# The opening of a fused attention and mixture-of-experts kernel, put in another order

## The reference, cut to what matters

```python
h = layernorm(x)                                  # no gain
qk, v = h @ Wqk, h @ Wv                           # split in heads of 16 channels
dot = qk_head @ qk_head.T                         # 16 x 16 for each head, summed over 2048 tokens
logits = (2 * dot - q2[:, None] - q2[None, :]) / sqrt(2048) * tau
out = (softmax(logits) @ v_head) -> tokens x 256, then @ Wo
x = x + layernorm(out)
h = layernorm(layernorm(x)) * ln_g + ln_b
expert(h) = (silu(h @ W1) * (h @ W3)) @ W2        # shared for all tokens, routed for the top two
x = x + layernorm(shared(h) + gated sum of the two routed experts, with a capacity)
```

## Time and profile before

| what | value |
|---|---|
| median of 3 runs | 1089.59 us (1089.08 to 1089.89) |
| profiled execution | 1089.17 us, its span 1087.4 us |
| TensorE busy | 1047.9 us, 96% of the span |
| VectorE, ScalarE, GpSimd busy | 656.2, 503.7, 385.4 us |
| granted TensorE clock over the span | 0.992 |

### The profile page before, as it was taken

The page is one execution under the profiler, slowest core; times in us unless marked ns, Lnnn a source line. Parts: engine busy times, 40 slices in busy tenths (PEclk is TensorE's granted clock), DMA queues, the critical chain, the costliest instruction groups (busy, mean ns, idle before and its releaser), DMA issues.

```text
span 1087.4 us, 19513 instructions
## 1 busy us (share of the span) xinstructions
PE 1047.9 (96%) x6863; PEld 958.0 (88%) x6863; DVE 656.2 (60%) x1714; ACT 503.7 (46%) x895; POOL 385.4 (35%) x347
## 2 busy tenths in 40 slices
PE   7998999999999999999999999999999999999985
PEld 6886888888888888889887899999999999999875
DVE  7768864677753678754786334545545463635686
ACT  4343444443434444353463334554546363545475
POOL 3112561114640104640117631434433343211385
PEclk9999999999999999999999999999999999999988
DMA  8222460242540234461134214434334242333799
GB/s 289 104 98 78 132 219 17 82 155 95 167 148 20 79 125 138 150 210 39 59 136 161 103 33 157 133 67 112 88 90 109 65 124 56 77 89 94 262 220 171
DMA packets 47229, 129.15 MB, mean 119 GB/s; under 512 B 10276, under 2 KB 17576, under 8 KB 47152
## 3 DMA queue, kind: packets, MB, share of 16 engines
q1 hardware_dynamic: 28656, 92.83, 25.5%
q0 software_dynamic: 18496, 35.35, 14.3%
HBM read 73.72 MB, written 54.40 MB: 118 GB/s over the span
## 4 chain that ended last, share of the span: by engine, by line
PE 82%; DVE 8%; POOL 4%; issue 3%; ACT 1%; DMA 1%; DVEq 0%; POOLq 0%; SPq 0%; ACTq 0%
PE bank L1136 25%; PE bank L1138 25%; PE bank L1137 25%; PE bank L1155 2%; POOL out_dram L906 2%; POOL sb_place_of L911 1%; DVE sb_stX L1427 1%; PE bank L1262 1%; PE bank L1315 1%; DVE sb_act L1734 1%; PE bank L1215 1%; PE bank L1274 1%; ACT sb_ln_o L965 1%; DMA sb_ysb<-in_L_ffn_W2s_dram 1%; PE bank L1185 1%
## 5 line engine op out<-in xcount | busy, mean ns | idle before, releaser
L1734 DVE TENSOR_TENSOR sb_act<-bank,sb_act 128x512 f32<-128x512 f32 (+2 forms) x240 | 148.6, 619 | 347.8 <-PE bank L1138 330.5
L1136 PE MATMUL bank<-sb_h_hi,sb_wup_lo 128*128 128x512 f32 (+2 forms) x960 | 354.7, 369 | 3.3 <-ACT sb_act L1061 2.1
L1138 PE MATMUL bank<-sb_h_hi,sb_wup_hi 128*128 128x512 f32 (+2 forms) x960 | 350.0, 365 | 0.0
L1137 PE MATMUL bank<-sb_h_lo,sb_wup_hi 128*128 128x512 f32 (+2 forms) x960 | 349.7, 364 | 0.0
L1061 ACT ACTIVATE sb_act<-bank 128x512 f32<-128x512 f32 (+2 forms) x240 | 129.8, 541 | 378.1 <-PE bank L1138 358.4
L1136 PE MATMUL bank<-sb_wdn_hi,sb_act_lo 128*128 128x256 f32 (+1 forms) x848 | 245.5, 290 | 5.1 <-ACT sb_ysb L1043 4.4
L1138 PE MATMUL bank<-sb_wdn_hi,sb_act_hi 128*128 128x256 f32 (+1 forms) x848 | 239.2, 282 | 0.0
L1137 PE MATMUL bank<-sb_wdn_lo,sb_act_hi 128*128 128x256 f32 (+1 forms) x848 | 239.0, 282 | 0.0
L1136 PEld LDWEIGHTS bank<-sb_h_hi,sb_wup_lo 128*128 128x128 f32 x960 | 181.0, 189 | 24.4 <-DVE sb_act L1734 2.5
L1138 PEld LDWEIGHTS bank<-sb_h_hi,sb_wup_hi 128*128 128x128 f32 x960 | 180.6, 188 | 22.6
L1137 PEld LDWEIGHTS bank<-sb_h_lo,sb_wup_hi 128*128 128x128 f32 x960 | 181.2, 189 | 17.1
(11 more groups left out here) (265 smaller groups left out, 1238.5 us busy)
## 6 DMA issues: line engine op xcount, KB each, us to landing
sb_xin<-in_L_ffn_W_dram SPq DMA_DIRECT2D x28, 512.0 KB, 3.6
sb_x<-in_L_attn_x_dram SPq DMA_DIRECT2D x16, 512.0 KB, 3.7
out_dram<-sb_x SPq DMA_DIRECT2D x16, 512.0 KB, 3.4
sb_xin<-in_L_attn_x_dram SPq DMA_DIRECT2D x14, 512.0 KB, 4.6
sb_xin<-in_x_turned_dram SPq DMA_DIRECT2D x14, 512.0 KB, 4.3
y_scratch<-sb_ysb SPq DMA_DIRECT2D x14, 512.0 KB, 4.2
sb_xn<-in_L_ffn_W_dram SPq DMA_DIRECT2D x14, 512.0 KB, 4.4
hT_scratch<-sb_hr SPq DMA_DIRECT2D x12, 512.0 KB, 2.7
```

Source lines behind the costliest of these rows:

```text
L1136: t_.matmul(o, a_lo, b_hi, start=start, stop=False, skip_group_check=True)
L1137: t_.matmul(o, a_hi, b_lo, start=False, stop=False, skip_group_check=True)
L1138: return t_.matmul(o, a_hi, b_hi, start=False, stop=stop, skip_group_check=True)
L1734: v.tensor_tensor(act[:, m % 3, 0:c.w], bank[(4 if c.wide and m % 2 else 0) + 1][:, 0:c.w], act[:, m % 3, 0:c.w], ALU.mult).then_inc(act_o ...
```

## The change

On TensorE, Wv's product leaves the head of the queue and becomes the step `wv_turn`, in two halves, at places 27 and 31 behind the Gram product; it reads Wv from another buffer and writes bank 1. In its old place stand 75 small products of ones. The counts of small products change: `m_dots` (18) and `m_rowdiag` (40) have none, the second half of `wv_turn` has 12. ScalarE copies `wvT` in `wv_keep`, at place 33.

For batch 0, VectorE normalizes tiles 0 and 1 of each group and makes a bias from mean and scale; ScalarE normalizes tiles 2 and 3 (`x_norm` on ScalarE). The Gram product waits tile by tile. The first group of x is loaded in two halves.

`x_keep` moves to places 13, 18, 27, 29 (from 16, 18, 24, 26); `x_low` to 17, 24, 35 and, for the fourth, to place 2 of step 0 (from 19, 20, 34, 34). `w_first` moves to 17, 21, 26, 28, 37, 37 (from 17, 19, 19, 29, 33, 34), `w_first_low` to 19, 24, 34, 44, 45, 47 (from 19, 24, 24, 34, 38, 38), `scale_taus` to 23 (from 25).

For step 0, ScalarE and VectorE share the first tile of h in another way, and the first row's products come as eight with the high part of h, then four with the remainder (`first_up`).

```diff
--- before.py
+++ after.py
...
@@ -456,7 +462,7 @@
         X_FIRST_AT = (("x_stats", (8, 9, 11, 13)), ("x_norm", (10, 12, 14, 15)), ("x_gram", (10, 12, 14, 15)),
-                      ("x_turned", (14, 14, 14, 15)), ("x_keep", (16, 18, 24, 26)), ("x_low", (19, 20, 34, 34)))
+                      ("x_turned", (14, 14, 14, 15)), ("x_keep", (13, 18, 27, 29)), ("x_low", (17, 24, 35, BEFORE + 2)))
         M_FIRST_AT = (20, 22, 22, 23, 24, 25, 26, 28, 30, 31, 32, 33, 34, 35, 36, 36, 37)
@@ -477,10 +483,12 @@
         put(0, -BEFORE, 0, zip(M_STEPS, M_FIRST_AT))
-        put(0, -BEFORE, 0, [("scale_taus", 25)])
-        for j, at in enumerate((17, 19, 19, 29, 33, 34)):
+        put(0, -BEFORE, 0, [("scale_taus", 23), ("wv_keep", 33)])
+        put(0, -BEFORE, 0, [("wv_turn", 27)])
+        put(0, -BEFORE, 1, [("wv_turn", 31)])
+        for j, at in enumerate((17, 21, 26, 28, 37, 37)):
             put(0, -BEFORE, j, [("w_first", at)])
-        for j, at in enumerate((19, 24, 24, 34, 38, 38)):
+        for j, at in enumerate((19, 24, 34, 44, 45, 47)):
             put(0, -BEFORE, j, [("w_first_low", at)])
@@ -534,8 +542,9 @@
         def _(sp):
-            for k in range(2):
-                sp.dma_start(x2[:, k, :, :], x_t[k]).then_inc(xres_in[k], 16)
+            for landed, tiles in ((x_early, slice(0, GT // 2)), (xres_in[0], slice(GT // 2, GT))):
+                sp.dma_start(x2[:, 0, tiles, :], x_t[0][:, tiles, :]).then_inc(landed, 16)
+            sp.dma_start(x2[:, 1, :, :], x_t[1]).then_inc(xres_in[1], 16)
             for opened in (hT_ok, g_done, o_ok, m_act, lno_ok, x2_ok, *x2_out, u_ok, ut_ps, lg_ps,
...
@@ -925,6 +933,16 @@
+            def x_norm(b, q):
+                if b > 0:
+                    return
+                act_e.wait_ge(x_nb, q + 1)
+                x = x2[:, q, :, :] if q < 2 else xin[:, q % 2, :, :]
+                for t, done in ((2, xn_third), (3, xn_ok)):
+                    s.activation(xnorm[q % 2][:, t, :], x[:, t, :], ACT.Identity, scale=rstdX[:, q, t:t + 1],
+                                 bias=nbX[:, q % 2, t:t + 1]).then_inc(done, 1)
             def x_high(b, q):
@@ -968,26 +986,35 @@
+            def first_keep(k):
+                act_e.wait_ge(ut_ps, OPEN + k + 1)
+                act_e.wait_ge(vec_in, 48)
+                s.activation(h_hi[:, shared_chunk(0, 0).slot, k, :], bank[6 + k][:, :], ACT.Identity,
+                             scale=gcol[:, k:k + 1], bias=bcol[:, k:k + 1]).then_inc((first_hi, hhi_ok)[k], 1)
+                if k == 1:
+                    s.activation(hfull[:, 1, :], bank[7][:, :], ACT.Identity,
+                                 scale=gcol[:, 1:2], bias=bcol[:, 1:2]).then_inc(hT_ok, 1)
             def u_keep(k):
                 def step(b, q):
-                    if opens(b, q) and k == 1:
+                    if opens(b, q):
+                        first_keep(k)
                         return
...
                     act_e.wait_ge(lg_ps, OPEN + b * GB + q)
-                    if b == 0 and q == 0:
-                        act_e.wait_ge(vec_in, 48)
                     if q == 0:
...
                         act_e.wait_ge(h_out, OPEN + b * H_LOADS + 16 * (q - 1))
-                    if opens(b, q):
-                        s.activation(h_hi[:, shared_chunk(0, 0).slot, 0, :], bank[6][:, :], ACT.Identity,
-                                     scale=gcol[:, 0:1], bias=bcol[:, 0:1]).then_inc(first_hi, 1)
                     s.activation((hfull if q == 0 else hr)[:, k, :], bank[6 + k][:, :], ACT.Identity,
...
-            steps = {"x_high": x_high, "x_keep": x_keep, "m_gram": m_gram,
+            def wv_keep(b, q):
+                act_e.wait_ge(wvT_ps, KC)
+                s.activation(wvT[:, :, :].rearrange("p k d -> p (k d)"), bank[1][:, :], ACT.Copy).then_inc(wvT_ok, 1)
+            steps = {"x_norm": x_norm, "wv_keep": wv_keep, "x_high": x_high, "x_keep": x_keep, "m_gram": m_gram,
                      "m_keep_t": m_halves(tsb, (5, 4), 2, (1, 0)),
...
@@ -1143,10 +1162,10 @@
                 for t in range(GT):
-                    if b == 0 and t < GT - 1:
-                        pe.wait_ge(xn_tile, q * (GT - 1) + t + 1)
+                    if b == 0 and t < GT // 2:
+                        pe.wait_ge(xn_tile, q * (GT // 2) + t + 1)
                     elif b == 0:
-                        pe.wait_ge(xn_ok, OPEN + (q + 1))
+                        pe.wait_ge((xn_third, xn_ok)[t - 2], (0, OPEN)[t - 2] + (q + 1))
                     for k in range(KC):
...
@@ -1316,12 +1333,29 @@
+            def first_up(c):
+                pe.wait_ge(first_hi, 1)
+                pe.wait_ge(w_lo, 4)
+                for k, turned in ((0, first_hi), (1, hhi_ok)):
+                    pe.wait_ge(turned, 1)
+                    for which in range(2):
+                        for w in (wup_lo, wup_hi):
+                            t_.matmul(bank[which][:, :], w[c.wset][:, which, k, 0:P], h_hi[:, c.slot, k, :],
+                                      start=(k == 0 and w is wup_lo), stop=False, skip_group_check=True)
+                for k, rest in ((0, first_lo), (1, hlo_ok)):
+                    pe.wait_ge(rest, 1)
+                    for which, full in ((0, a_ps), (1, b_ps)):
+                        ins = t_.matmul(bank[which][:, :], wup_hi[c.wset][:, which, k, 0:P], h_lo[:, c.slot, k, :],
+                                        start=False, stop=(k == KC - 1), skip_group_check=True)
+                        if k == KC - 1:
+                            ins.then_inc(full, 1)
             def up(c, m, first_wide):
-                opening = isinstance(c.n, int) and c.n == 0 and m == 0
-                if opening:
-                    pe.wait_ge(first_lo, 1)
-                    pe.wait_ge(w_lo, 4)
-                elif m == 0:
+                if isinstance(c.n, int) and c.n == 0 and m == 0:
+                    first_up(c)
+                    return
+                if m == 0:
                     pe.wait_ge(hlo_ok, c.n + 1)
...
@@ -1371,13 +1403,20 @@
+            ONES_MADE = 4
+            pe.wait_ge(const_ok, ONES_MADE)
+            for _ in range(75):
+                t_.matmul(bank[0][:, 0:P], onesb[:, :], onesb[:, :], start=True, stop=True)
             pe.wait_ge(const_ok, NCONST)
-            pe.wait_ge(wv_in, 16)
-            for k in range(KC):
+            def wv_turn(b, k):
+                if k == 0:
+                    pe.wait_ge(wv_in, 16)
                 for c in range(KC):
-                    ins = t_.matmul(bank[6][:, k * D:(k + 1) * D], tsb[:, c, k * P:(k + 1) * P], center[:, c, :],
+                    ins = t_.matmul(bank[1][:, k * D:(k + 1) * D], wv[:, c, k * P:(k + 1) * P], center[:, c, :],
                                     start=(c == 0), stop=(c == KC - 1))
-            ins.then_inc(wvT_ps, 1)
+                ins.then_inc(wvT_ps, 1)
+            steps["wv_turn"] = wv_turn
             def keep_clock(step, n):
@@ -1387,7 +1426,7 @@
             opening_steps = dict(steps)
-            for name, n in (("m_times_wqk", {(0, 0): 3}), ("m_dots", {(0, 0): 18}), ("m_rowdiag", {(0, 0): 40}),
+            for name, n in (("m_times_wqk", {(0, 0): 3}), ("wv_turn", {(0, 1): 12}),
                             ("m_times_wo", {(0, 0): 3}), ("m_times_wv", {(0, 0): 6}), ("o_mix", {(0, 1): 25, (0, 2): 35}),
@@ -1435,13 +1474,18 @@
             def x_stats(b, q):
-                if b == 0 and q < 2:
-                    dve.wait_ge(xres_in[q], 16)
+                if b == 0 and q == 0:
+                    dve.wait_ge(x_early, 16)
+                elif b == 0 and q == 1:
+                    dve.wait_ge(xres_in[1], 16)
                 else:
...
                 x = x_from(b, q)
-                stats(ch, lambda t: x[:, t, :], stX[:, q % 2, :, :], mvX[:, q % 2, :, :])
+                def half(t):
+                    if b == 0 and q == 0 and t == GT // 2:
+                        dve.wait_ge(xres_in[0], 16)
+                stats(ch, lambda t: x[:, t, :], stX[:, q % 2, :, :], mvX[:, q % 2, :, :], half)
                 v.tensor_scalar(veX[:, q, :], mvX[:, q % 2, :, 1], EPS, None, ALU.add).then_inc(a_var, 1)
@@ -1452,13 +1496,17 @@
                     dve.wait_ge(xlo_ok, OPEN + g - GB - 1)
-                for t in range(GT):
+                for t in range(GT if b > 0 else GT // 2):
                     ins = v.tensor_scalar(xnorm[q % 2][:, t, :], x_from(b, q)[:, t, :], mvX[:, q % 2, t, 0:1],
-                                          rstdX[:, q % 2, t:t + 1],
+                                          rstdX[:, q, t:t + 1],
                                           ALU.subtract, ALU.mult)
-                    if b == 0 and t < GT - 1:
+                    if b == 0:
                         ins.then_inc(xn_tile, 1)
-                ins.then_inc(xn_ok, 1)
+                if b == 0:
+                    v.scalar_tensor_tensor(out=nbX[:, q % 2, :], in0=mvX[:, q % 2, :, 0], scalar=-1.0,
```

(23 more changed lines are left out.)

19 lines of the change are left out of this document (5 added, 14 removed).

## The result

Nine runs of the changed kernel have a median of 1092.96 us (1090.55 to 1095.49), nine of the kernel before beside them 1089.4. The ratio is 1.0031, 95% interval 1.0021 to 1.0042: 3.4 us slower, where no change (1089.6) was forecast and the range ended at 1091.4. A second set gave 1.003 (1.0018 to 1.0042). The profiled execution took 1093.01 us, its span is 1091.3; before they were 1089.17 and 1087.4. So the trace has 3.8 us to explain.

A forecast was written before the change was run, and what follows sets the result against it. TensorE holds 82% of the chain that ended last, so only its stalls or useless work count. Gram -1.4, W2 -1.2, powers +1.65, step 0 +1.4 sum to +0.45 on 1089.17: 1089.6 us, range 1087.3 to 1091.4.

The forecast's parts named there:

- The Gram term: Opening, Gram product on TensorE: fourth group ends at 19.65 instead of 21.03, a gain of 1.4 us (1.1 to 1.5).
- The rival of a turned x that lands later: Opening: the turned x lands later and the Gram gain shrinks to 0.3 from 1.4, 1090.7 us; chance 0.10.
- the sum: All terms together: -1.4 - 1.2 + 1.65 + 1.4 = +0.45 us on the profiled 1089.17, giving 1089.6.
- W2: ScalarE's wait for a piece of W2 ahead of the mixing product's copy goes: 1.2 us gained (0.9 to 1.3).
- Powers: VectorE's remainder subtractions beside GpSimd's two powers make each end 0.90 later: 1.65 us lost (0 to 2 x 0.90).
- Step 0: TensorE's product at 61.75 comes 1.4 us later: 1.13 from the fourth x remainder, 0.27 from the first step's product order.
- The clock's rival: Thinner opening: longer TensorE pauses drop its clock to half, 1.7 us a spell, 1091.3 or 1093.0; chance 0.09.

The follow-up runs named there:

- a2: Changed kernel with ScalarE's copy of the first turned x at place 16, behind the fourth group's normalization, instead of 13; ratio 1.0035.
- a0: The changed kernel itself, run again with nothing changed; ratio 1.0030.
- a4: Changed kernel with W3's remainder moved to place 38 and W2's second to place 49, away from GpSimd's powers; ratio 1.0021.
- a3: Changed kernel with the fourth x remainder on VectorE at place 38 instead of in step 0; ratio 1.0019.
- a1: Changed kernel with the first group of x loaded in one DMA again; ratio 1.0018.
- b1: Kernel before with ScalarE's two copies of W2's pieces at place 37, as in the changed kernel; ratio 0.9999.
- c2: a5 with the old order of the first step; ratio 0.9997.
- d4: c2 with 8 instead of 36 small products behind the transposes of the first tile; ratio 0.9986.
- c1: a5 with 8 instead of 36 small products behind the transposes of the first tile; ratio 0.9990.
- d2: Kernel before with a5's places of x_keep, x_low, w_first, w_first_low and scale_taus, without the Gram part; ratio 0.9992.
- a5: Changed kernel with all four repairs, the edits of a1, a2, a3 and a4, together; ratio 0.9998.

## Why the prediction was wrong

**The Gram term is the step that failed.** It was put at -1.4, from "one more DMA issue", "0.1 to 0.15 of delay, as the queue was still full of x at that time". The queue was not indifferent: with the first x in two loads the third group landed 2.5 later and the first turned x 2.2 later, and the term came out at +0.85. That is 2.25 of the 3.4 us by which the forecast missed the trace. The price was taken from SyncE's issue time alone; the landing was never bounded from both sides. The rival of a turned x that lands later had half of the place (in a2 the turned x was out of the way, and the third group still held VectorE), but kept a gain of 0.3, and had a chance of 0.10. The Trainium skill, Perfetto Trace Analysis, section "DMA Optimizations", says that splitting DMAs may let some start sooner and the whole complete sooner if the DMA engines are generally idle. They were not idle here: from 3 to 7 us their share was 1.02 in the kernel before. The first half did land 0.9 sooner; what stood behind it landed later.

The term is not one number, either. In the four traces with the changed kernel's Gram part the copy came at 22.08, 22.39 (a0), 21.07 (a4) and 19.62 (a3), which is +0.85, +1.16, -0.16 and -1.61 against 21.23. So where the loads landed as the sum assumed, in a3, its gain was there, and a little more. It had "Halving the first load starts VectorE earlier; nothing on the path waits for that", but in a3 TensorE began its first group 0.7 ahead of a1, which loads the first x whole.

Without the split the term is -1.0 (a1). The sum had followed ScalarE's third group and ended at 19.5; TensorE's own four groups it counted only from the end of the small products, taken at about 8. With x whole they begin at 9.1 to 9.3, behind VectorE's first normalization and the statistics of two groups, and 9.2 + 4 x 2.73 = 20.1.

**Not in the sum:** +0.32 between the Gram copy and the product at 29.56, and +0.65 behind step 0 (0.28 of it the longer wait at 590.49). The prediction had put both at nothing. Of the 0.32, 0.24 is a gap of VectorE ahead of the taus' table at 23.48, for which the trace names no releaser.

**The other terms held.** W2: -1.16 for -1.2, though b1 shows that it is a gain only with the remainders gone. Powers: 1.92 and 1.91 as the earlier trace rows had it, +1.56 for +1.65; a4 returned both. The Trainium skill's rule (SBUF — State Buffer, section "SBUF: two separate sides"), by which the two would have cost 2.1, agrees in kind; the 0.91 and 0.90 measured are a little less. Step 0: +1.61 for +1.4, of which a3 returned 1.2 and c2 0.22. The clock's rival did not occur in the changed kernel: the pause ahead of 30.73 was 1.15 and nothing fell before the fall that was there already. But in its second profiled execution (a0, 1096.14 us) the clock fell once more, behind a pause of 2.03 ahead of 592.10, so the clock can have a part in single runs. With the Gram term at its measured +0.85 and the 0.32, the sum is +3.0, and 1092.2, 0.8 below the profiled run.

**The lowest ratio** among these is d4's: all four repairs, the old first step and 8 small products, 0.9986 (0.9977 to 0.9995), 1.5 us below the kernel before. The intervals of c1 and d2 overlap it.

## What to carry to other kernels

A load split in two for an early start is to be priced by when everything behind it in the queue lands, not by its issue. Work given to an idle engine pushes back what that engine did next: list its queue up to the next copy on which the path waits. And a gain of a microsecond in an opening can be lost again at a far pause: in a5 and c2 a load landed later there, TensorE waited longer, and its clock fell.
